# One transformer block on one core: c and the first modulation rows loaded from ScalarE's queue, scale and shift rows as two products

## The reference, cut to what matters

```
x: (1024, 256); c: (1, 256); wmod: (256, 6 * 256)
mod = silu(c) @ wmod                      # six rows of 256: sa, ca, ga, sb, cb, gb
h   = layernorm(x) * (1 + ca) + sa        # ca: first scale row, sa: first shift row
x   = x + ga' * attention(h)              # attention begins with a layernorm of h, then q, k, v
h   = layernorm(x) * (1 + cb) + sb
x   = x + gb' * moe(h)                    # 32 experts, 4 for each token, and a shared expert
```

## Time and profile before

| | |
|---|---|
| time, median of 3 runs | 152.6 us (152.41 to 152.67) |
| the profiled execution: span from first to last instruction | 161.2 us |
| the profiled execution's own time outside that span | not recorded |
| PE busy | 145.7 us (90%) |
| DVE busy | 111.7 us (69%) |
| ACT busy | 65.0 us (40%) |
| POOL busy | 48.5 us (30%) |
| chain that ended last: PE, DVE, issue | 51%, 26%, 7% of the span |

### The profile page before, as it was taken

How to read it: one execution, slowest core, us unless ns; L and a number is a source line. 1 busy time by engine, 2 the same in 40 slices (tenths; PEclk the granted TensorE clock), 3 DMA queues, 4 the chain that set the end, 5 groups by cost and what they waited for, 6 DMA issues and landing times.

```text
span 161.2 us, 2747 instructions
## 1 busy us (share of the span) xinstructions
PE 145.7 (90%) x915; PEld 105.2 (65%) x915; DVE 111.7 (69%) x394; ACT 65.0 (40%) x173; POOL 48.5 (30%) x71
## 2 busy tenths in 40 slices
PE   7889799999999999999999999717997989699992
PEld 7846548468566775898787887404564555368881
DVE  2848989898986497798759824107672949559994
ACT  3233680486155428749879411101232323131000
POOL 7400004279520000002000077773176536500000
PEclk9999999999999999999999999995699999999999
DMA  4999999999999997001003034543014011159983
GB/s 114 277 385 387 418 418 375 349 348 348 352 348 350 347 349 242 1 28 51 0 5 109 2 76 117 116 116 94 0 47 105 33 48 45 47 151 343 406 283 134
DMA packets 22080, 31.28 MB, mean 194 GB/s; under 512 B 2065, under 2 KB 18231, under 8 KB 22066
## 3 DMA queue, kind: packets, MB, share of 16 engines
q1 hardware_dynamic: 20642, 27.71, 50.6%
q0 software_dynamic: 1424, 3.39, 7.8%
HBM read 23.65 MB, written 8.13 MB: 197 GB/s over the span
## 4 chain that ended last, share of the span: by engine, by line
PE 51%; DVE 26%; issue 7%; another core or an unknown queue 5%; DMA 4%; ACT 4%; SPq 1%; DVEq 0%
PE bank L1638 8%; PE bank L1445 7%; PE score_pair L1497 5%; PE bank L1660 4%; PE score_pair L1423 4%; PE score_pair L1419 4%; DMA w_sb<-in_L_wmod_dram 4%; PE bank L1497 3%; PE bank L1432 2%; PE score_pair L1445 2%; DVE base L1262 2%; PE score_pair L1651 2%; DVE aT L853 2%; PE score_pair L1295 2%
## 5 line engine op out<-in xcount | busy, mean ns | idle before, releaser
L1638 PE MATMUL bank<-w_sb,arena 128*64 128x256 f32 x128 | 18.3, 408 | 1.3 <-issue 1.2
L500 POOL DMA_INDIRECT arena<-token_rows,gather_idx x16 | 16.1, 1009 | 10.3 <-DVE gather_idx L1046 5.8
L509 POOL DMA_INDIRECT results<-arena,res_idx x11 | 11.0, 999 | 13.3 <-DVE arena L1181 10.9
L1445 PE MATMUL bank<-arena 128*128 128x256 f32 x56 | 13.7, 382 | 0.2 <-ACT arena L602 0.2
L1638 PEld LDWEIGHTS bank<-w_sb,arena 128*64 128x64 f32 x128 | 9.0, 145 | 7.5 <-issue 5.2
L473 POOL TENSOR_TENSOR base<-aT,mod 128x256 f32<-128x256 f32 x8 | 5.8, 726 | 24.3 <-DVE aT L857 20.6
L1445 PEld LDWEIGHTS bank<-arena 128*128 128x128 f32 x56 | 10.1, 190 | 2.3 <-issue 1.3
L593 ACT ACTIVATE prob<-score_pair,nmax 128x128 f32<-128x128 f32 (+7 forms) x8 | 5.9, 742 | 11.6 <-DVE nmax L930 11.5
L1651 PE MATMUL score_pair<-ident,h2T 128*128 128x128 f32 x16 | 3.7, 319 | 7.5 <-DVE base L1063 4.3
L1423 PE MATMUL score_pair<-arena 128*128 128x512 f32 (+3 forms) x24 | 10.1, 504 | 0.0
L1419 PE MATMUL score_pair<-arena 128*128 128x512 f32 (+3 forms) x24 | 9.8, 490 | 0.0
(11 more groups left out here) (223 smaller groups left out, 345.4 us busy)
## 6 DMA issues: line engine op xcount, KB each, us to landing
w_sb<-in_L_ffn_w_dram SPq DMA_DIRECT2D x12, 1024.0 KB, 12.5
results<-prob SPq DMA_DIRECT2D x1, 4096.0 KB, 15.8
w_sb<-results SPq DMA_DIRECT2D x6, 512.0 KB, 7.9
token_rows<-rows SPq DMA_DIRECT2D x8, 144.0 KB
xin<-in_L_attn_x_dram SPq DMA_DIRECT2D x4, 256.0 KB, 6.4
w_sb<-in_L_wmod_dram SPq DMA_DIRECT2D x1, 1024.0 KB, 9.5
out_dram<-base SPq DMA_DIRECT2D x8, 128.0 KB, 2.3
w_sb<-in_L_attn_qkv_dram SPq DMA_DIRECT2D x1, 768.0 KB, 7.6
```

The costliest lines, as they stand in the source:

```text
L500: nc.gpsimd.indirect_dma_start(out=slot_in[:, r, :], out_offset=None, in_=rows_d, in_offset=bass.IndirectOffsetOnAxis(ap=gather_idx[:, r:r ...
L509: nc.gpsimd.indirect_dma_start(out=results_d, out_offset=bass.IndirectOffsetOnAxis(ap=res_idx[:, r:r + 1], axis=0), in_=ob[g % 4][:, (r % ...
L1445: last = t.matmul(PV_BANK[i][:, 0:H], probT[:, i % 2, j, :], vo[:, j, :], start=(j == 0), stop=(j == i))
L1638: last = t.matmul(bank[4 + g % 2][CAP * side:CAP * side + CAP, 2 * F * r:2 * F * r + 2 * F], slotT[:, k, CAP * e:CAP * e + CAP], w13_sb[:, ...
```

## The change

c is issued first from ACT's queue instead of SP's. ACT then loads its table, and issues the scale columns of wmod and the shift columns of wmod as two transfers of 256 KB, each with a semaphore. SP's queue then begins with x; qkv follows the first two pairs of x directly, and o_proj moves up behind `wmod_b`, ahead of the last two pairs of x and the small loads. The product of 512 columns becomes two of 256, scale first, in banks 0 and 7. ACT copies the shift row into SBUF after the third weight copy and after the first four tiles of h are done; `make_h(4, 4)` reads that copy. The 72 small products have 96 columns instead of 128.

```diff
         @block.sync
-            sp.dma_start(cc[:, 0, :], c.rearrange("a (p k) -> p (a k)", k=KT)).then_inc(c_loaded, 16)
             for j in range(NB):
                 sp.dma_start(xin[:, 2 * j:2 * j + 2, :], x_d[:, 2 * j:2 * j + 2, :]).then_inc(x_loaded[j], 16)
                 if j == 1:
-                    sp.dma_start(wmod_a, wmod_d[:, :, 0:512]).then_inc(wmod_loaded[0], 16)
                     sp.dma_start(qkv_sb, qkv.rearrange("(p k) n -> p k n", k=KT)).then_inc(qkv_loaded, 16)
                     sp.dma_start(wmod_b, wmod_d[:, :, 512:1536]).then_inc(wmod_loaded[1], 16)
+                    sp.dma_start(wo_sb, o_proj.rearrange("(j p) n -> p j n", p=P)).then_inc(wo_loaded, 16)
...
-            sp.dma_start(wo_sb, o_proj.rearrange("(j p) n -> p j n", p=P)).then_inc(wo_loaded, 16)
...
         @block.scalar
+            act.dma_start(cc[:, 0, :], c.rearrange("a (p k) -> p (a k)", k=KT)).then_inc(c_loaded, 16)
             a.add_instruction(mybir.InstLoadActFuncSet(
...
+            first_mod = wmod.rearrange("(p k) n -> p k n", k=KT)
+            act.dma_start(wmod_a[:, :, H:2 * H], first_mod[:, :, H:2 * H]).then_inc(scale_loaded, 16)
+            act.dma_start(wmod_a[:, :, 0:H], first_mod[:, :, 0:H]).then_inc(wmod_loaded[0], 16)
...
             wT_evac(2)
+            act.wait_ge(h_dve, 4)
+            a.copy(mod[:, 0, :], SHIFT_BANK[:, 0:H]).then_inc(shift_copied, 1)
             rsqrt_seed(1)
...
             def make_h(first, count):
-                dve.wait_ge(mod_mm, 1)
+                dve.wait_ge(scale_mm, 1)
...
+                dve.wait_ge(mod_mm, 1)
+                if first:
+                    dve.wait_ge(shift_copied, 1)
                 for i in tiles:
-                    v.tensor_tensor(h[:, i, :], h[:, i, :], bank[0][:, 0:H], ALU.add).then_inc(h_dve, 1)
+                    v.tensor_tensor(h[:, i, :], h[:, i, :], mod[:, 0, :] if first else SHIFT_BANK[:, 0:H], ALU.add).then_inc(h_dve, 1)
...
+            def first_mod_row(m):
+                return product((SHIFT_BANK if m == 0 else SCALE_BANK)[:, 0:H],
+                               [(silu_c[:, k, :], wmod_a[:, k, H * m:H * m + H]) for k in range(KT)])
...
-                    t.matmul(bank[1][:, 0:P], ones_bf[:, :], ones_bf[:, :], start=True, stop=True)
+                    t.matmul(bank[1][:, 0:96], ones_bf[:, :], ones_bf[:, 0:96], start=True, stop=True)
...
             pe.wait_ge(silu_c_done, 1)
+            pe.wait_ge(scale_loaded, 16)
+            first_mod_row(1).then_inc(scale_mm, 1)
             pe.wait_ge(wmod_loaded[0], 16)
-            mod_rows(0)
+            first_mod_row(0).then_inc(mod_mm, 1)
```

More of the change, by code:

```diff
@@ L210, in adaln_attention_moe @@
         wmod_loaded = [sem("wmod_loaded0"), sem("wmod_loaded1")]
+        scale_loaded = sem("scale_loaded")
         qkv_loaded = sem("qkv_loaded")
@@ L232, in adaln_attention_moe @@
         silu_c_done = sem("silu_c_done")
+        scale_mm = sem("scale_mm")
         mod_mm = sem("mod_mm")
         mod_raw = sem("mod_raw")
+        shift_copied = sem("shift_copied")
         gagb_done = sem("gagb_done")
@@ L357, in adaln_attention_moe @@
         POS, SLOTS = 128, (256, 256 + 2 * PAIRS)
-        MOD_BANK = [bank[0], bank[2]]
+        SCALE_BANK, SHIFT_BANK, GATE_BANK = bank[0], bank[7], bank[2]
         block = ctx.enter_context(nc.Block())
@@ L564, in mod_evac @@
                 act.wait_ge(mod_mm, 2)
-                a.copy(mod[:, 2::3, :], MOD_BANK[1][:, :].rearrange("p (m n) -> p m n", m=2)).then_inc(mod_raw, 1)
+                a.copy(mod[:, 2::3, :], GATE_BANK[:, :].rearrange("p (m n) -> p m n", m=2)).then_inc(mod_raw, 1)
             def hn_tile(i):
@@ L852, in make_h @@
                         dve.wait_ge(xhat_done, sum(j not in XHAT_DVE for j in range(i + 1)))
-                    step(v.scalar_tensor_tensor(out=h[:, i, :], in0=bank[0][:, H:2 * H], scalar=1.0, in1=h[:, i, :],
+                    step(v.scalar_tensor_tensor(out=h[:, i, :], in0=SCALE_BANK[:, 0:H], scalar=1.0, in1=h[:, i, :],
                                                 op0=ALU.add, op1=ALU.mult))
                 settle()
+                dve.wait_ge(mod_mm, 1)
+                if first:
+                    dve.wait_ge(shift_copied, 1)
                 for i in tiles:
-                    v.tensor_tensor(h[:, i, :], h[:, i, :], bank[0][:, 0:H], ALU.add).then_inc(h_dve, 1)
+                    v.tensor_tensor(h[:, i, :], h[:, i, :], mod[:, 0, :] if first else SHIFT_BANK[:, 0:H], ALU.add).then_inc(h_dve, 1)
                 dve.wait_ge(h_dve, first + count)
@@ L1296, in product, with gate_rows @@
                 return last
[L1299 to L1302, removed]
+            def first_mod_row(m):
+                return product((SHIFT_BANK if m == 0 else SCALE_BANK)[:, 0:H],
+                               [(silu_c[:, k, :], wmod_a[:, k, H * m:H * m + H]) for k in range(KT)])
+            def gate_rows():
+                w = wmod_b.rearrange("p k (m n) -> p k m n", n=H)[:, :, 0::3]
+                product(GATE_BANK[:, :].rearrange("p (m n) -> p m n", n=H),
                         [(silu_c[:, k, :], w[:, k]) for k in range(KT)]).then_inc(mod_mm, 1)
@@ L1504, in _ @@
             pe.wait_ge(wmod_loaded[1], 16)
-            mod_rows(1)
+            gate_rows()
             fold_vo(0)
```

## The result

The changed kernel took 153.97 us (median of four runs, 152.93 to 155.12) where the kernel before took 152.5 (150.87 to 152.67): ratio 1.0132, 95% interval 1.0071 to 1.0193. Medians in this document are of all runs, but ratios leave out the runs that lie more than 1.5% above the fastest of their kernel, and the profiled runs of e1, e3 and e6 are among those, so their spans are not compared. The forecast was 151.8 and faster; the change made the kernel slower, by about what the rival "shift half late" had been priced at, 154.0.

What follows compares the result with a forecast made beforehand. PE's line from qkv's landing was taken as the bound past 0.48 us of DVE's gain. turn_h(0) gains 0.92 us, 0.87 in timed runs; with a tenth for new waits, 152.5 becomes 151.8 us, range 151.0 to 153.4.

Steps and rivals of the forecast that it cites:

- shift half late: Slower rival: queues alternate unequal pieces, shift half lands at 11.4, PE loses 1.5 us; 154.0 us, or 153.2; chance 0.26.
- The shift half: Shift columns on ACT's queue beside qkv: landed at 8.8, product ready at 9.9, DVE gains 1.9 us to normalized h.
- The prediction's own sign of being wrong: In the profile after, the shift product would end after qkv's landing.
- c leaves SP's queue: x, qkv and later loads are issued 0.44 us earlier; qkv lands at 10.1 instead of 10.5, gain bounds 0 to 2.4.
- c on ACT's queue: c's issue precedes ACT's table load; the row issues run beside that load, so nothing changes for exp(-c).
- Even the second stays under the bound below: If issues wait for the table load, exp(-c) starts at 3.4, normalized x stands at 8.9 instead of 8.14; still covered.
- Warm-up products: The 72 narrower products on PE end between 6.0 and 7.6 us, near the scale half's landing; effect taken as nothing.
- The scale half: Scale columns on ACT's queue land at 7.0, product ready at 8.1, DVE begins multiplies at 8.2 instead of 10.43.
- the bound: Past 0.48 us of DVE's gain, PE's line, beginning with qkv's landing, limits the start up to turn_h(0).
- the turn at 16.5: turn_h(0) on PE starts at 16.5 instead of 17.42, waiting for PE's own stream; gain 0.92 us.
- the copy of the shift row: ACT's copy into SBUF, 0.36 us, ends at 13.1 before the moments at 13.3; cost nothing, without idle time 0.36.
- a third of 0.20: Rival of nothing at the end, 152.5 us, chance 0.20, a third still a gain; the sum of faster counted 0.04.

Runs made afterwards that it cites:

- e1: The changed kernel with c alone moved back to the front of SP's queue: 152.42 us, ratio 1.0006 to the kernel before.
- e3: The changed kernel with c and both halves of wmod's rows on SP's queue, c ahead of x: 151.69 us, ratio 0.9963 to the kernel before.
- e6: The changed kernel with the shift row's product moved behind qkv's twelve transposes on PE: 153.5 us, ratio 1.0077 to the kernel before.
- e4: The changed kernel unaltered, run again on another comparison's chip: 155.12 us, ratio 1.0186 to the kernel before.
- e5: The changed kernel with GpSimd's memset held until silu(c) is done: 154.67 us, ratio 1.0111 to the kernel before.
- e11: The changed kernel with 60 more unread products on PE ahead of the wait for the shift half: 153.34 us, ratio 1.0072 to the kernel before.
- e9: The changed kernel with only the shift half moved to SP's queue, ahead of qkv: 151.91 us, ratio 1.0009 to the kernel before.
- e2: The changed kernel with scale and shift halves on SP's queue ahead of qkv, c still on ACT's: 151.39 us, ratio 0.9969 to the kernel before.
- e7: e8 with the first two turns of h on PE ahead of the gate rows and fold_vo(0): 152.59 us, ratio 1.0050 to the kernel before.
- e8: The changed kernel with both halves on SP's queue ahead of qkv and the memset held until silu(c): 150.71 us, ratio 0.9903 to the kernel before.
- e10: The changed kernel with wmod_b and o_proj issued behind x pairs 3 and 4: 153.27 us, ratio 1.0042 to the kernel before.

## Why the prediction was wrong

**The step that failed** is "The shift half": "With equal shares both move 512 KB, at 265 to 342 GB/s some 1.8 us: landed at 8.8, product ready at 9.9." The shares were equal in packets, not in bytes, and not with qkv. qkv, issued 0.15 us earlier with three times the bytes, went ahead and was through at 7.5; the shift half's packets began at 6.0, got a fifth of the bytes beside `wmod_b`'s (0.16 MB of 0.80 from 7 to 9 us), and it landed at 10.1 (10.9 to 11.4 in e4, e5, e6 and e11). PE waits for it in order, ahead of the transposes, so its landing became the head of PE's line. The prediction's own sign of being wrong came: the shift product ended at 11.66, after qkv's landing. e9, which changes nothing but this one transfer's queue, takes the loss away.

The prediction had set 9.9 as the landing from which the slower rival decides, and that is how it came. The rival's mechanism, turns with pieces of unequal size, was right by the packets from 7 to 9 us (156 against 161), but its partner was `wmod_b` where the rival counted qkv's pieces first. That 153.97 met its price of 154.0 so closely is luck: the price set the landing 1.3 us later than the first profile has it, and left out the clock, 1.2 us by e11. I gave it too small a chance because the row that I held against it, "small and issued early", speaks only within one queue.

**"c leaves SP's queue", "I move its landing by 0.44 alone"** mis-sized qkv's landing: 10.1 forecast, 7.5 measured (8.1 to 9.0 in e4, e5, e6 and e11). The bytes that went ahead of it were not the same, since the shift half came behind it; in e9, where the half goes ahead, qkv landed at 9.3. This gain lay ready and could not be used, as PE stood before the shift half's wait.

**"c on ACT's queue", "I take the first"** was wrong by another road than the one weighed. The issues did run beside the table load (L533 and L534 at 1.31 and 1.95, the load from 1.28 to 2.56), but c itself took 3.0 us to land where it had taken 1.8 at the front of SP's queue (2.4 in e2, e7 and e8, where ACT's queue held c alone). That put the work on c beside GpSimd's memset, which cost 1.5 us more. Together this made x's moments 2.4 us later and ate what the early scale row had given. The prediction's line "Even the second stays under the bound below" priced a delay of 0.8 us.

**"Warm-up products", "I take nothing"** left out PE's idle time. The warm-up ended at 5.6, the scale product at 7.63, and after the gap from there to 10.13 the granted clock was 0.50. By e11 this cost about 1.2 us of the path to `xn1_evac`.

**"The scale half"** came near with its product, ready at 7.63 against 8.1 forecast, by luck: it landed at 5.4 instead of 7.0, its packets ahead of qkv's, but the product then waited for silu(c) to 6.50. It changed nothing, as DVE had no x to multiply.

**Right** were the bound (PE's line, e7), the turn at 16.5 once the transfers allow it (e8), the copy of the shift row (0.38 us at 14.81, before the seed that starts at 15.15, with no wait put on it), and that what the start loses or gains is carried to the gather (73.6 to 73.9 us from `xn1_evac` on, in all runs but e7). A slip in the chances changes none of this: a third of 0.20 is 0.07, not the 0.04 of the sum, and 0.26 less 0.03 is 0.23, not 0.24.

Settled is thus where the loss comes from: the late shift half (e9, e6), with the clock as a part of its price (e11), and c with the memset as the reason why no gain stood against it (e5, e8, e9). How the two queues share once both move is shown by the packet counts of after and e10. Still open are why the shift half's packets begin only at 6.0, and why c takes 3.0 us behind ACT's other issues.

## What to carry to other kernels

A transfer that is moved to a second queue need not keep its place: here the shift half landed at 10.1 on ACT's queue and at 7.1 on SP's (e9). Price its share in packets and not in bytes (here 1 KB against 4 gave a fifth of the bytes), reckon with what was issued just ahead of it on the other queue going first (here qkv, issued 0.15 us earlier, landed 2.6 us before it), and look for the landing from which the engine waiting in order on it becomes the bound. Here a wait of PE for 256 KB stood ahead of work whose data had been there for 2.5 us; put the transfer that an in-order engine wants first into the same queue as the next one, ahead of it (e9, 1.0009 where after has 1.0132 and 1.0186). And when a small step moves by a microsecond, look at what it will run beside in its new place (here 1.65 us beside the memset instead of 0.17).

## What was not expected of the hardware

- A 128x2 operation of DVE took 1.60 to 1.90 us instead of 0.17 when it ran beside GpSimd's memset of 128x2048 (after, e4, e6, e9, e10, e11), and in e2 the 128x256 copy behind it 1.81 instead of 0.29; with the memset held back 0.17 and 0.29 (e5).
- Of two transfers issued 0.15 us apart on two queues, the one of 768 KB landed 2.6 us before the one of 256 KB; it took 5.7 us from issue to landing itself, where it took 7.6 in the one queue of before.
- From 7 to 9 us of after two queues moved packet for packet, 156 against 161, with 4 KB in the one's packets and 1 KB in the other's. From 5 to 6 us, with the shift half issued at 1.95, they did not: 61 against none.
- After 2.5 us without products the granted clock was 0.50 for about 3 us (after), and so after 2.12 us in e10; after 1.66 us (e8) it stayed at 1.00, with eight transposes in 1.09 us. The length of one idle stretch does not sort the runs: in e6 eight transposes ran as fast after 1.43 us, and after a second idle stretch of 1.1 us the clock was 0.50 from 12 to 14 us.
